# Latent key values loaded in two halves, and GpSimd's gathers and row additions dealt out over other slots, in a four-part transformer kernel

## The reference, cut to what matters

```python
x = x + _L0_xattn_ref(_layernorm(x), ...)
# (2): routed is the sum over a row's 4 chosen experts, each times its share
x = x + (routed + sg * shared)
# (3): 16 heads; keys and values come from a latent kv_c of 64 values a row
kv_c = kv @ W_kvc                        # 1024 x 64
k_rope = _rope(kv_c @ W_kr, lk)
q_c = q @ W_dq                           # q is the layer norm of x after (2)
scores = (q_nope . k_nope + q_rope . k_rope) * scale, masked to 9 key numbers
out = softmax(scores) @ v @ W_o
x = x + out
x = x + _L1_ffn_ref(_layernorm(x), ...)
```

## Time and profile before

| | |
|---|---|
| median of 3 runs | 577.43 us (573.11 to 577.86) |
| the profiled execution | 575.07 us |
| its span, first to last instruction | 573.3 us |
| PE busy | 494.4 us (86% of the span) |
| DVE, ACT, POOL busy | 446.2, 354.0, 330.8 us |
| mean granted TensorE clock | 0.956 |

### The profile page before, as it was taken

How to read it: one execution, slowest core, us unless ns; L and a number is a source line. 1 busy time by engine, 2 the same in 40 slices (tenths; PEclk the granted TensorE clock), 3 DMA queues, 4 the chain that set the end, 5 groups by cost and what they waited for, 6 DMA issues and landing times.

```text
span 573.3 us, 11091 instructions
## 1 busy us (share of the span) xinstructions
PE 494.4 (86%) x3338; PEld 435.4 (76%) x3338; DVE 446.2 (78%) x1373; ACT 354.0 (62%) x909; POOL 330.8 (58%) x316
## 2 busy tenths in 40 slices
PE   0699979999799999995658999999999998578894
PEld 0488757877698998983448999999999997346673
DVE  4789956976879898856658788889899985859674
ACT  2345446343567675763237887878788889657643
POOL 2547661014368886325798899898767872353100
PEclk9999998999999999995588999999999999789997
DMA  8144554312364657646720010100000000000000
GB/s 279 39 125 132 147 138 120 88 55 65 106 202 113 193 170 196 163 132 165 244 51 29 20 29 19 29 20 1 3 0 2 2 2 2 0 1 11 9 29 27
DMA packets 27960, 45.24 MB, mean 79 GB/s; under 512 B 5696, under 2 KB 18848, under 8 KB 27264
## 3 DMA queue, kind: packets, MB, share of 16 engines
q1 hardware_dynamic: 21056, 28.15, 16.1%
q0 software_dynamic: 3792, 10.74, 7.8%
q10 hardware_dynamic: 3056, 5.65, 2.9%
HBM read 34.63 MB, written 8.85 MB: 76 GB/s over the span
## 4 chain that ended last, share of the span: by engine, by line
PE 51%; DVE 20%; POOL 10%; issue 9%; ACT 5%; DMA 4%; SPq 0%; ACTq 0%; DVEq 0%; POOLq 0%
PE bank L422 8%; PE bank L1098 8%; PE bank L424 8%; PE bank L423 8%; PE bank L1540 5%; POOL yk L619 2%; PE bank L1300 2%; PE bank L1302 2%; PE bank L1301 2%; PE bank L1495 2%; POOL Q_lo L668 1%; POOL Q L662 1%; DVE X L1651 1%; POOL pr L655 1%; DVE asel L1651 1%
## 5 line engine op out<-in xcount | busy, mean ns | idle before, releaser
L591 POOL DMA_INDIRECT inb<-rows_kept,row_of x47 | 46.9, 998 | 34.3 <-PE bank L1098 19.8
L974 ACT ACTIVATE pr<-sc,smin 128x256 f32<-128x256 f32 x128 | 63.3, 503 | 0.0
L668 POOL TENSOR_TENSOR Q_lo<-Q,Q_hi 128x512 fp32r<-128x512 f32 x32 | 41.5, 1297 | 15.9 <-ACT Q_hi L719 14.9
L2110 DVE CUSTOM_DVE_ANT_0 sc<-bank,bias 128x256 f32<-128x256 f32 x128 | 46.6, 419 | 0.1
L1599 DVE TENSOR_TENSOR pT_lo<-bank,pT_hi 128x512 fp32r<-128x512 f32 x64 | 41.1, 683 | 6.2 <-ACT pT_hi L719 6.0
L719 ACT ACTIVATE pT_hi<-bank 128x512 fp32r<-128x512 f32 x64 | 34.8, 595 | 14.8 <-PE bank L1098 14.4
L422 PE MATMUL bank<-K_hi,Q_hi 128*128 128x256 f32 x128 | 37.7, 295 | 5.4 <-POOL Q_lo L668 5.4
L549 POOL TENSOR_TENSOR Wd<-wd_raw,Wd 128x512 fp32r<-128x512 f32 x13 | 16.8, 1289 | 42.3 <-ACT Wd L766 42.2
L662 POOL TENSOR_TENSOR Q<-Q,rot 128x512 f32<-128x512 f32 x32 | 41.1, 1284 | 0.0
L655 POOL TENSOR_TENSOR pr<-pr,srec 128x512 f32<-128x512 f32 x32 | 33.3, 1040 | 12.5 <-DVE srec L2117 12.4
L619 POOL DMA_INDIRECT yk<-slots_y,slot x32 | 32.4, 1013 | 10.8 <-issue 5.5
(11 more groups left out here) (350 smaller groups left out, 1946.7 us busy)
## 6 DMA issues: line engine op xcount, KB each, us to landing
slots_y<-yb SPq DMA_DIRECT2D x47, 128.0 KB
wg_raw<-gate_up_dram SPq DMA_DIRECT2D x22, 256.0 KB, 2.7
bw<-bits_dram ACTq DMA_DIRECT2D x3, 1024.0 KB
wd_raw<-down_dram SPq DMA_DIRECT2D x16, 128.0 KB, 2.2
wo<-wo_dram SPq DMA_DIRECT2D x2, 1024.0 KB, 6.6
wd_raw<-down_dram SPq DMA_DIRECT2D x30, 64.0 KB, 2.3
gu_raw<-gate_up_dram SPq DMA_DIRECT2D x6, 256.0 KB, 3.6
X<-x_dram SPq DMA_DIRECT2D x2, 512.0 KB, 6.6
```

Of the source, the lines that this page charges most:

```text
L591: pool.indirect_dma_start(inb[:, j % NIN, :], None, rows_d, bass.IndirectOffsetOnAxis(row_of[:, j:j + 1], 0)).then_inc(slots_in[j % NIN], 16)
L668: pool.tensor_tensor(Q_lo[:, i % 2, :], Q[:, i % 2, :], Q_hi[:, i % 2, :].bitcast(F32), ALU.subtract).then_inc(queries_low_g, 1)
L974: e = act.activation(pr[:, i % 2, z, :], sc[:, i % 2, z, :], ACT.Exp, bias=smin[:, i % 2, z:z + 1], scale=-1.0, accum_out=ssum[:, i % 2, z ...
L2110: dve.tensor_tensor_reduce(sc[:, r, z, :], bank[2 + h][:, u * S:(u + 1) * S], bias[:, TB * b_ + u, :], 1.0, 3.0e38, ALU.add, ALU.min, smin ...
```

## The change

1. **Latent in two halves.** `kvT_hi` and `kvT_lo` (high and low part, all 1024 columns) become `kvT0` and `kvT1`: each holds the high and the low part of 512 columns. The two loads of `kvT0` are issued in SP's store loop after store 43, after waiting until all slot tiles are turned and their shares computed; `qr` is loaded after store 41 and not 42. The two loads of `kvT1` stand where the whole loads stood. K(0,·) waits for `kvT0` alone; the transposes V0 and V1 read both.
2. **DVE's order before the loop.** The units K(1,·) come ahead of `combine(0)`; `bq_lo` moves from before `norm3(1)` to after the second `sin2` operation.
3. **POOL's order before the loop.** `power2(0)`, the gathers of tile 2, `power2(1)`, the gathers of tile 3. A gather of tile 4 and later waits for the rows added on POOL and not for DVE's moments.
4. **POOL's tables in the loop.** The three additions of tile 2 come before slot 0, those of tile 3 in slots 0 and 1; gathers start in slot 0 and are spread otherwise, two of them in slots 7 and 16; additions are one a slot in most. `MOMENTS` of tiles 0 to 3 move from slots 14, 15, 22, 23 to 17, 18, 24, 25, `QUANTISE` of tiles 0 to 3 from 18, 24, 26, 27 to 22, 26, 27, 28.

```diff
-        FETCH = {i: (4 + (i - 1) // TOPK, (i - 1) % TOPK) for i in range(1, 1 + 4 * TOPK)}
-        ADD_ROWS = {0: ((2, 0), (2, 1), (2, 2)), 1: ((3, 0), (3, 1), (3, 2)), 6: ((4, 0),), 7: ((4, 1), (4, 2)), 9: ((5, 0),),
-                    10: ((5, 1), (5, 2)), 14: ((6, 0),), 15: ((6, 1), (6, 2)), 17: ((7, 0),), 18: ((7, 1), (7, 2))}
-        COMBINE = {1: 2, 2: 3, 8: 4, 11: 5, 16: 6, 19: 7}
-        MOMENTS = {14: 0, 15: 1, 22: 2, 23: 3, 29: 4, 30: 5}
-        QUANTISE = {18: 0, 24: 1, 26: 2, 27: 3, 31: 4, 32: 5}
+        FETCH = {0: ((4, 0),), 1: ((4, 1),), 2: ((4, 2),), 3: ((4, 3),), 5: ((5, 0),), 6: ((5, 1),), 7: ((5, 2), (5, 3)),
+                 9: ((6, 0),), 10: ((6, 1),), 11: ((6, 2),), 12: ((6, 3),), 14: ((7, 0),), 15: ((7, 1),), 16: ((7, 2), (7, 3))}
+        ADD_ROWS = {-1: ((2, 0), (2, 1), (2, 2)), 0: ((3, 0),), 1: ((3, 1), (3, 2)), 4: ((4, 0),), 5: ((4, 1),), 6: ((4, 2),),
+                    8: ((5, 0),), 9: ((5, 1),), 10: ((5, 2),), 13: ((6, 0),), 14: ((6, 1),), 15: ((6, 2),),
+                    17: ((7, 0),), 18: ((7, 1), (7, 2))}
+        COMBINE = {1: 2, 2: 3, 7: 4, 11: 5, 16: 6, 19: 7}
+        MOMENTS = {17: 0, 18: 1, 24: 2, 25: 3, 29: 4, 30: 5}
+        QUANTISE = {22: 0, 26: 1, 27: 2, 28: 3, 31: 4, 32: 5}
...
-                if j == 42:
+                if j == 41:
                     sp.dma_start(qr[:, :, :], qr_d).then_inc(uq_in, 16)
+                if j == 43:
+                    sp.wait_ge(slots_turned_p, TILES)
+                    sp.wait_ge(slot_share_v, TILES)
+                    for x in range(2):
+                        sp.dma_start(kvT0[:, x, :].bitcast(F32), kv_keep[x, :, 0:HALF]).then_inc(kv_kept, 16)
             sp.wait_ge(mask_g, 3 * NT)
-            sp.dma_start(kvT_hi[:, :].bitcast(F32), kv_keep[0]).then_inc(kr_in, 16)
-            sp.dma_start(kvT_lo[:, :].bitcast(F32), kv_keep[1]).then_inc(kr_in, 16)
+            for x in range(2):
+                sp.dma_start(kvT1[:, x, :].bitcast(F32), kv_keep[x, :, HALF:N]).then_inc(kr_in, 16)
...
-            power2(0)
-            power2(1)
-            for t in range(TB, 2 * TB):
+            for t in range(TB):
+                power2(t)
                 for k in range(TOPK):
-                    gather(t, k)
+                    gather(TB + t, k)
...
             pool.wait_ge(x_shared_v, NT)
+            for t, step in ADD_ROWS[-1]:
+                add_rows(t, step)
...
-                    pe.wait_ge(kr_in, 48)
+                    if n == 0:
+                        pe.wait_ge(kv_kept, 64)
+                    else:
+                        pe.wait_ge(kr_in, 48)
...
             for ab in range(2):
                 prepare(PREP.index(("K", 0, ab)))
+            for ab in range(2):
+                prepare(PREP.index(("K", 1, ab)))
             combine(0)
             moments3(0)
-            for ab in range(2):
-                prepare(PREP.index(("K", 1, ab)))
...
             norm3(0)
-            lo(bq_lo[:, :, :], qrs[:, :, :], bq_hi[:, :, :]).then_inc(small_low_v, 1)
             norm3(1)
             lo_h(1, 0, bank[4], G_lo, G_hi)
             link(dve.tensor_scalar(sin2[:, 0, :], sin1, upper[:, :], None, ALU.mult))
             lo_h(1, 1, bank[5], G_lo, G_hi)
             dve.tensor_tensor(sin2[:, 1, :], sin1, sin2[:, 0, :], ALU.subtract)
+            lo(bq_lo[:, :, :], qrs[:, :, :], bq_hi[:, :, :]).then_inc(small_low_v, 1)
             lo_q(0, bank[6][:, 0:S])
```

More of the change, by code:

```diff
@@ L227, in build @@
                        {"skip": ([P, 5120], F32), "G_hi": ([P, KD, N], F32R), "G_lo": ([P, KD, N], F32R),
-                        "yk": ([P, 2, TOPK, D], F32), "kvT_hi": ([KVC, N], F32R), "kvT_lo": ([KVC, N], F32R)},
+                        "yk": ([P, 2, TOPK, D], F32), "kvT1": ([KVC, 2, HALF], F32R), "kvT0": ([KVC, 2, HALF], F32R)},
                        {"skip": ([P, 11264], F32), "xr": ([P, NT, D], F32)}))
@@ L243, in build @@
             "gsil hid gu_hi gu_lo dn_hi dn_lo logit rmax prob rsum top8 topix onehot member").split()]
-        (bits, bias, yb, bw, xT_hi, xT_lo, dT_hi, dT_lo, sil, hd, sbias, uq, uk, G_hi, G_lo, yk, inb, kvT_hi, kvT_lo, xr) = [
-            m[k] for k in ("bits bias yb bw xT_hi xT_lo dT_hi dT_lo sil hd sbias uq uk G_hi G_lo yk inb kvT_hi kvT_lo xr"
+        (bits, bias, yb, bw, xT_hi, xT_lo, dT_hi, dT_lo, sil, hd, sbias, uq, uk, G_hi, G_lo, yk, inb, kvT1, kvT0, xr) = [
+            m[k] for k in ("bits bias yb bw xT_hi xT_lo dT_hi dT_lo sil hd sbias uq uk G_hi G_lo yk inb kvT1 kvT0 xr"
                            ).split()]
@@ L346, in piece @@
             return slice(c * BANK, (c + 1) * BANK)
[L348 to L354 removed]
+        FETCH = {0: ((4, 0),), 1: ((4, 1),), 2: ((4, 2),), 3: ((4, 3),), 5: ((5, 0),), 6: ((5, 1),), 7: ((5, 2), (5, 3)),
[6 more added lines that the diff above has]
+        QUANTISE = {22: 0, 26: 1, 27: 2, 28: 3, 31: 4, 32: 5}
+        NORMS = [(2, 0), (2, 1), (2, 2), (2, 3), (2, 4), (2, 5), (2, 6), (3, 0), (3, 1), (2, 7), (3, 2), (3, 3), (3, 4),
                  (3, 5), (3, 6), (3, 7)]
@@ L615, in gather @@
             def gather(t, k):
-                if t >= 2:
+                if 2 <= t < 4:
                     pool.wait_ge(variance_v, norm_count(2, t - 2))
+                elif t >= 4:
+                    pool.wait_ge(rows_added_g, 3 * (t - TB - 1))
                 z = TOPK * t + k
@@ L696, in _ @@
                     add_rows(t, step)
-                if i in FETCH:
-                    gather(*FETCH[i])
+                for t, k in FETCH.get(i, ()):
+                    gather(t, k)
                 if i - 1 in MOMENTS:
@@ L1159, in prepare @@
                     _, n, ab = unit
-                    pe.wait_ge(kr_in, 48)
+                    if n == 0:
+                        pe.wait_ge(kv_kept, 64)
+                    else:
+                        pe.wait_ge(kr_in, 48)
                     pe.wait_ge(small_low_v, 1)
-                    cols = slice(n * HALF, (n + 1) * HALF)
-                    e = split3(pe, b[:, :], kr_hi[:, ab, :], kr_lo[:, ab, :], kvT_hi[:, cols],
-                               kvT_lo[:, cols], True, True)
+                    part = (kvT0, kvT1)[n]
+                    e = split3(pe, b[:, :], kr_hi[:, ab, :], kr_lo[:, ab, :], part[:, 0, :], part[:, 1, :], True, True)
                 elif unit[0] == "V":
-                    part = (kvT_hi, kvT_lo)[unit[1]]
                     pe.wait_ge(slots_copied_a, TILES)
                     for t in range(NT):
-                        e = pe.transpose(b[:, t * KVC:(t + 1) * KVC], part[:, t * P:(t + 1) * P].bitcast(F32),
-                                         ident[0:KVC, 0:KVC])
+                        n, x = divmod(t, NT // 2)
+                        e = pe.transpose(b[:, t * KVC:(t + 1) * KVC],
+                                         (kvT0, kvT1)[n][:, unit[1], x * P:(x + 1) * P].bitcast(F32), ident[0:KVC, 0:KVC])
                 elif unit[0] == "M":
```

## The result

The kernel after took 572.91 us in the median of 22 runs (569.02 to 577.62); the kernel before, on the same chip, 576.74 (571.71 to 584.47). The ratio is 0.9941 with a 95% interval of 0.9919 to 0.9963: 3.4 us less (2.1 to 4.7). That is faster, but by under 1%, and the median lies 0.5 us above the 572.4 forecast. The experiments ran on three chips, each beside the kernel before on its own chip.

What follows compares the result with a forecast made beforehand. PE was taken to bound the steady loop and POOL's list the way into it. Terms 2.4 + 0.3 + 1.4 + 1.2 - 0.3 = 5.0 us off 577.43 gave 572.4 us, range 567.5 to 577.0.

Steps and rivals of the forecast that it cites:

- Latent sooner: Before the loop: `kvT0` there before PE wants it, second half landing about 4 us after issue, K(0,·) off the path.
- Part 3, `power2(1)` and `norm3(1)`: Before the loop: `power2(1)` at 273.5 to 274.8 against 273.90; `norm3(1)` 0.5 us sooner, from 0.9 gain to 0.3 loss.
- Part 3, `q_add(0)`: POOL before the loop: four gathers fewer behind `power2(1)`, so `q_add(0)` starts 2.4 us sooner, bounds 1.5 and 3.0.
- Part 4, slots 0 to 3: POOL's first loop slots: 0.3 us saved in slot 0, 1.4 in slot 1; `q_lo(3)` 4.1 us sooner in all.
- Steady waits: Loop after slot 4: 1.2 us of PE's waits for `share01` back, bounds 0 and 1.7, less 0.3 for quantisations.
- The third `scale_x` in a row: Slots 26 to 28: three in a row can run DVE late, costing 0.3 us, bounds 0 and 1.5.
- Rival (d): From `turn_p(0)`: longer gap drops PE to its lower clock, whole slots slow, 587.9 us; chance 0.07.
- Part (a): Way into the loop: shorter gaps spare PE the lower clock, 1.15 us, POOL's terms high; 569.9 us, chance 0.30.
- Stores: SP's store loop: two load issues ahead of stores 44 to 46 delay them by 0, at worst 0.9 us.
- The rule weighed: Gathers before the loop: the skill's DVE and GpSimd port lock, by which tile 2's gathers would stretch beside `combine(1)`.
- Rival (b): Before the loop: each gather of tile 2 takes 0.67 us more, the 2.4 are lost; 575.0 us, chance 0.10.

Runs made afterwards that it cites:

- e1_half: Kernel before with only the latent loaded in two halves, orders and tables unchanged; 576.04 us against 577.11, ratio 0.9982.
- e10_old_warm: Kernel before with 18 extra PE matmuls filling the gap in front of `turn_p(0)`; 575.07 us, ratio 0.9989 to before.
- e4_bq: Kernel after with `bq_lo` moved back between `norm3(0)` and `norm3(1)`; 571.93 us, ratio 0.9913 to before.
- e3_tables: Kernel before with only after's loop tables, additions of tile 2 ahead of slot 0 included; 577.86 us, ratio 1.0013 to before.
- e5_quant: Kernel after with `QUANTISE` of tiles 1 to 3 in slots 24, 26, 27, so never three in a row; 572.35 us, ratio 0.9937 to before.
- e12_after: Kernel after, unchanged, run once more on another chip; 573.54 us, ratio 0.9934 to before.
- e2_pre: Kernel after with before's loop tables and no additions ahead of slot 0; 574.90 us, ratio 0.9960 to before.
- e9_all: Kernel after with `bq_lo` back, quantisations in slots 22, 24, 26, 27, and 24 plus 44 filler matmuls; one run 567.86 us, five 577.4 to 580.3, no ratio.

## Why the prediction was right, and where its terms were off

The verdict held (3.4 us of 5.0 forecast, under 1%). The gain shows in the profile at the steps named, with two terms too high and one too low. That the time itself was met to 0.5 us is in part luck: the forecast started from 577.43, the median of three runs, and 22 runs gave 576.74, 0.7 lower, which hid as much of the gain that was missing. All that follows is from the profiles of before and after:

- **Latent sooner.** Right. PE's wait fell from 4.2 to 0.3 us. The half issued at 258.88 was used at 262.58, 3.7 later; I took 4. What this is worth in time is not shown: e1_half alone gains nothing that can be told.
- **Part 3, `power2(1)` and `norm3(1)`.** Right. `power2(1)` came 22.90 after the clearing, 22.71 before; `norm3(1)` 23.52 against 24.02, the 0.5 us that I took. Against e10_old_warm, which is before's program up to there, nothing is left of it: `norm3(1)` came at 23.56 there.
- **Part 3, `q_add(0)`: the step that failed.** 2.4 us forecast, bounds 1.5 and 3.0; measured 34.43 - 33.12 = 1.31, and 0.8 to 2.0 between any two profiles of the two programs. "Four gathers with one stretched, 5.5" was wrong: from 278.09 to 284.68 they took 6.6. Two were stretched, by 0.8 and 1.0: I let `bq_lo` (1.22 us, two SBUF inputs) go "into a gap" and asked only who waits for it, not whom it blocks, and the gather under the two `K_lo`, which I had counted as the one stretched, started nearer to their start (0.16 us behind it, 0.48 before). e4_bq shows that block by moving it. The trace of before had it already: the prediction puts the gather at 274.74 (1.43) beside `norm3(1)`, but `bq_lo` had begun before that gather and `norm3(1)` after it. That DVE's input came no sooner did not matter: it was there at 286.43, 1.1 before POOL.
- **Part 4, slots 0 to 3.** 0.3 and 1.4 forecast; 0.44 and 1.33 measured. But slot 3 lost 0.33, since POOL now waits for ACT's `Q_hi` before `q_lo(3)` (0.37, shown above), which I had called an input that comes earlier. Together with 0.03 lost in slot 2, `q_lo(3)` moved 2.72 us, not 4.1 (2.3 to 3.5 between any kernel with after's program up to there and either with before's: 51.12 to 51.87 against 54.15 and 54.59).
- **Steady waits.** 1.2 back and 0.3 against, so 0.9 forecast; the rest without slot 4 shrank by 1.52, and with the tables alone (e3_tables) by 1.61. This excess offsets part of what `q_add(0)` fell short. In 340 to 480 us the waits for `share01` went from five of 1.7 to two of 0.8. The third `scale_x` in a row stalls PE by about 1 us as was feared, but e5_quant shows that undoing it gains nothing net, so that rival is out.
- **The clock.** Rival (d)'s mechanism was there at small scale: 1.38 us more in slot 4, no second slot; 0.96 by e12_after. Part (a)'s claim that shorter gaps spare PE the lower level failed; the longest gap grew from 2.38 to 3.64 as said against it. But the gap's length does not decide alone: e4_bq had 3.63 and a slot 4 of 6.64, e1_half 2.40 and 7.93.
- **Stores.** 0 forecast, worst 0.9; measured 0.34 between the two profiles, 1.0 in e1_half and e2_pre, 1.2 in e9_all.

The sum of the profiles: 1.31 + 0.44 + 1.33 - 0.03 - 0.33 - 1.38 + 1.52 = 2.86 us, all from the clearing of `V_hi`, the 0.34 of the stores being inside the first term. The range 567.5 to 577.0 held the result.

**The rule weighed.** Rival (b) had all four gathers of tile 2 stretched by 0.67; they lasted 1.00, 1.06, 0.96 and 0.95, so it fell. But what it names, a gather stretched by DVE, is what cost most of the missing 1.1 us, behind `power2(1)`. The Trainium skill ("SBUF — State Buffer", Who interferes with whom) says that DVE with two SBUF inputs contends with GpSimd's reads and that the order of issue decides who blocks; the rows at 280.66, 282.71 and 270.46 agree on both counts. The same section infers that a `tensor_tensor` does not hold up the making of descriptors, which needs the write interface; here the rows differ, 1.75 us against 0.95 beside `bq_lo`, and the rows decide. That the lock is the mechanism is the page's statement; the runs show when a gather waits and how long, not on what. The row at 265.90, which I read as evidence against it, only showed a gather that had started first.

## What to carry to other kernels

When an instruction is moved into a gap, ask not only who waits for it but what other engines will start during it. In these kernels a GpSimd gather of 0.95 us that starts inside a two-input DVE instruction ends about 0.83 us after it. A part of a change on one serial list can be worth nothing without another: here the tables alone left POOL's list as long as it was and one gather longer. Whether the timed gains add up is not shown, since the intervals of e2_pre and after overlap. And compare two profiles from the last common event before the change, since here the parts in front of it differed by more than the change was worth.
